# How many queued FFN steps go into each gap of the attention chunks: half of the per-chunk budget instead of a third

## The reference, cut to what matters

```python
q = elu_feature_map(proj(Wq)); k = elu_feature_map(proj(Wk)); v = proj(Wv)
# per token i, 16 heads of 64:
kv_sum = kv_sum + einsum('bhd,bhe->bhde', k_i, v_i); k_sum = k_sum + k_i
out_i  = einsum('bhd,bhde->bhe', q_i, kv_sum) / (sum(q_i * k_sum) + EPS)
x = layernorm(x + out @ Wo.T)
h = layernorm(x) * gamma + beta
y = silu(h @ dequant(fc1_q, fc1_scales) + fc1_bias)      # 1024 -> 4096
z = y @ dequant(fc2_q, fc2_scales) + fc2_bias            # 4096 -> 1024
x = layernorm(x + (x + 0.5 * z))
```

## Time and profile before

| what | value |
|---|---|
| median of 2 timed runs | 3252.29 us |
| the two runs | 3212.3 and 3292.28 us |
| the profiled execution, its time | 3161.46 us |
| its span (slowest core, core 1) | 3159.8 us |
| spans of the eight cores | 3141.0 to 3159.8 us |
| mean granted TensorE clock | 0.838 to 0.842 |
| prefix stage (to the first L690) | 521.8 us on core 1 |

### The profile page before, as it was taken

One profiled execution on the slowest core, in us unless ns is written; L12 is line 12 of the kernel. 1 busy time (PEld: TensorE's weight loads), 2 busy tenths in 40 slices (PEclk: granted clock), 3 DMA queues, 4 the chain that ended last, 5 costly groups with the idle time before them and its releaser, 6 DMA issues.

```text
span 3159.8 us, 31216 instructions; the slowest of 8 cores (3141.0 to 3159.8 us)
## 1 busy us (share of the span) xinstructions
PE 2089.2 (66%) x11268; PEld 957.4 (30%) x11268; DVE 1241.7 (39%) x1724; ACT 871.1 (28%) x1162; POOL 64.7 (2%) x126
## 2 busy tenths in 40 slices
PE   1777775666776667656765777566848674776385
PEld 0333332333332333233323333233323332333132
DVE  0555554444424432443244324334333343225314
ACT  0222222234212431143115311522152215222411
POOL 1000000000000000000000000000000000000000
PEclk9888887777798789968896889688968886888598
DMA  9677774000142113121312132321122213220241
GB/s 197 162 220 215 215 217 115 7 7 7 30 110 69 46 30 103 62 59 30 96 61 64 34 83 64 86 58 47 54 83 70 63 38 94 70 57 27 80 123 64
DMA packets 171884, 262.17 MB, mean 83 GB/s; under 512 B 40659, under 2 KB 114387, under 8 KB 169684
## 3 DMA queue, kind: packets, MB, share of 16 engines
q1 hardware_dynamic: 154164, 201.38, 22.8%
q0 software_dynamic: 17568, 58.79, 8.5%
HBM read 251.82 MB, written 33.55 MB: 90 GB/s over the span
## 4 chain that ended last, share of the span: by engine, by line
PE 48%; DVE 18%; DMA 13%; ACT 11%; issue 7%; another core or an unknown queue 2%; SPq 1%; DVEq 0%; ACTq 0%
PE PS L514 14%; PE PS L532 13%; PE PS L327 6%; DMA w1d<-wsl_a 5%; DMA w2d<-wsl_c 5%; PE PS L793 4%; DVE z_sb L543 3%; PE PS L690 3%; DMA out<-out_s 2%; DVE st_m L765 2%; ACT h_fm L472 2%; PE PS L760 2%; DVE r_s L552 1%; DVE u_s L548 1%
## 5 line engine op out<-in xcount | busy, mean ns | idle before, releaser
L532 PE MATMUL PS<-w2r_a,y_fm 128*128 128x512 bf16 x1024 | 280.0, 423 | 216.9 <-DVE z_sb L543 107.4
L327 PE MATMUL PS<-wqkv,x_fma 128*128 128x512 bf16 x1536 | 375.1, 402 | 25.7 <-DVE z_sb L543 7.1
L543 DVE TENSOR_TENSOR z_sb<-PS,z_sb 128x1024 f32<-128x1024 f32 x96 | 117.4, 1223 | 538.5 <-PE PS L532 513.4
L520 ACT ACTIVATE y_fm<-PS,b_s 128x512 bf16<-128x512 f32 x256 | 176.1, 688 | 519.0 <-PE PS L514 502.7
L514 PE MATMUL PS<-h_fm,w1r_a 128*128 128x512 bf16 x1024 | 258.9, 414 | 61.7 <-ACT y_fm L520 33.2
L532 PE MATMUL PS<-w2r_b,y_fm 128*128 128x512 bf16 x1024 | 252.9, 392 | 0.0
L514 PE MATMUL PS<-h_fm,w1r_b 128*128 128x512 bf16 x1024 | 236.7, 391 | 4.9 <-DVE st_m L765 3.0
L327 PEld LDWEIGHTS PS<-wqkv,x_fma 128*128 128x128 bf16 x1536 | 154.7, 102 | 244.3 <-issue 85.7
L532 PEld LDWEIGHTS PS<-w2r_a,y_fm 128*128 128x128 bf16 x1024 | 99.8, 105 | 383.2 <-issue 307.5
L514 PEld LDWEIGHTS PS<-h_fm,w1r_a 128*128 128x128 bf16 x1024 | 106.1, 105 | 210.0 <-issue 113.2
L711 PE MATMUL PS<-ident,khat 128*128 128x128 bf16 x256 | 27.7, 273 | 203.6 <-DVE khat L343 199.9
(11 more groups left out here) (141 smaller groups left out, 2422.0 us busy)
## 6 DMA issues: line engine op xcount, KB each, us to landing
w2r_a<-w2d SPq DMA_DIRECT2D x32, 1024.0 KB, 5.4
w2r_b<-w2d SPq DMA_DIRECT2D x32, 1024.0 KB, 7.5
out<-out_s SPq DMA_DIRECT2D x32, 512.0 KB, 2.9
s1b_a<-fc1sb SPq DMA_DIRECT2D x4, 2048.0 KB, 10.2
s2b_a<-fc2sb SPq DMA_DIRECT2D x16, 512.0 KB, 8.5
s2b_b<-fc2sb SPq DMA_DIRECT2D x16, 512.0 KB, 4.1
g1a<-fc1q POOLq DMA_DIRECT2D x4, 2048.0 KB, 11.3
g2a<-fc2q POOLq DMA_DIRECT2D x16, 512.0 KB, 5.1
```

The source lines that it names most:

```text
L327: op("tensor", lambda e, d=d, s=s, xfm=xfm: e.matmul(PS[g][:, 512 * s:512 * s + 512], xfm[:, 128 * d:128 * d + 128], wqkv[:, 3072 * d + D ...
L520: op("scalar", lambda e, m=m, lo=lo: e.activation(out=y_fm[:, 512 * (m % 8):512 * (m % 8) + 512], in_=PS0[:, lo:lo + 512], func=AF.Silu, b ...
L532: op("tensor", lambda e, m=m, s=s, rbuf=rbuf: e.matmul(PS0[:, 1024 + 512 * s:1536 + 512 * s], y_fm[:, 512 * (m % 8) + 128 * t: 512 * (m % ...
L543: op("vector", lambda e, t=t: e.tensor_tensor(out=z_sb[:, D * t:D * t + D], in0=PS0[:, 1024:2048], in1=z_sb[:, D * t:D * t + D], op=ALU.ad ...
```

## The change: half of the budget per slot

```diff
-            b3 = (budget + 2) // 3
+            b3 = (budget + 1) // 2
```

## The result

| | before | after |
|---|---|---|
| median | 3161.73 us (10 runs) | 3198.48 us (11 runs) |
| lowest to highest | 3156.63 to 3292.28 | 3191.07 to 3247.65 |
| profiled execution | 3161.46 us, span 3159.8 | 3190.32 us, span 3188.7 |
| ratio | | 1.0123, 95% interval 1.0089 to 1.0157 |
| granted clock | 0.838 to 0.842 | 0.837 to 0.841 |

The changed kernel is 1.2% slower: less than 2%, but the interval leaves out 1. The two runs of before that the prediction had (3212.3 and 3292.28) turned out to be the two highest of ten; the other eight lie between 3156.6 and 3181.6. Times as long as those two come, wherever the clock was recorded beside them, with a lower granted clock on the cores of a die (3217.3 us at 0.80, where the other die had 0.84), and such executions are left out of the ratios.

A forecast was written before the change was run, and what follows sets the result against it. The prediction took TensorE's work plus the idle stretches ahead of it as the bound. Its terms, 6.0 + 2.3 - 2.5 + 30.0 + 4.1 = +39.9 us, put on the median 3252.29, gave 3292 us, range 3195 to 3340.

The forecast's parts named there:

- round 3: Chunks 12 to 15, priced mostly by old chunks' windows: 326.7 us against 320.7, +6.0.
- round 7: Chunks 28 to 31: chunk 28 dearer, chunk 30 empty, a stall lost in 31; +4.1 us.
- Rounds 4 and 5: Each becomes the old round after it, item for item: +2.3 and -2.5 us.
- Round 6: Chunks 24 to 27, a new filling with nothing left to flush, walked slot by slot: 351.2 us against 321.2, +30.0.
- upper bound: Chunks 24 to 27 at old chunk 22's ratio to flush prices, 1.19: 356.6 us, so +35.
- fc2 pair at the start of the flush: Chunk 15's flush: first two fc2 take 10.1 + 6.4 us instead of 2 x 5.15, as z_sb waits behind layer norm.
- first fc1 of the flush: Chunk 15: leaves old chunk 15's flush, saving 13.9 us, as it waited behind the layer norm's ScalarE work.
- 1.5 because no flush lies ahead of final_block: Start of chunk 28: with no flush ahead to cover final_block's start, the chunk takes 1.5 us more.
- Rival 1: Filling slots pays: 21 FFN items leave the flushes, each hiding 1.8 us; -37 us, 3215; chance 0.08.
- Rival 2: It cancels: chunks 24 to 27 pay flush prices, +5, chunks 28 to 31 give nothing; +11 us, 3263; chance 0.17.
- Rival 3: 1 MB loads come 5.4 us late at six places, chunks 24 to 29: +72 us, 3324; chance 0.20, shared with longer VectorE chains.
- Whole rounds don't gain: TensorE's granted clock: single chunks gain from denser work, rounds 3 to 6 of before do not (0.85, 0.84, 0.84, 0.83).

The follow-up runs named there:

- round-6-only: Kernel before, with the new rule for items per slot used in chunks 24 to 27 alone; ratio to the kernel before 1.0101.
- all-but-round-6: Changed kernel, but chunks 24 to 27 keep the old rule for items per slot; ratio to the kernel before 1.0028.
- aligned kernel: Kernel before, re-dealt: each round's first chunk takes ten steps, the next three one FFN quarter each, the last quarter flushed; ratio 0.9587, repeated 0.9545.
- last experiment: Aligned kernel with one transposed h_fm tile moved from slot 4 to slot 5 in each round's first chunk; ratio to the kernel before 0.9423.
- last-quarter run: Changed kernel, but the last four fc2 of chunks 24 to 27 stay queued for the flush; ratio to the kernel before 1.0099.

## Why the prediction was right and where it was wrong

**The level was wrong, and that made the number wrong.** The failed step is "The two timed runs ... lie above that execution, with a median of 3252.29. I put the sum on the median: 3292 us". The sum of the steps on the profiled execution was 3201; the median measured is 3198.48, and the profiled execution after took 3190.32. The two timed runs at hand were the two highest of ten, and the kernel before has a median of 3161.73, within 0.3 us of its profiled execution. Against that, 3292 reads as +4.1%, which nothing in the working supports. The durations all came from the profiled execution, so the sum belonged on its time; three values spread over 4% (3161, 3212, 3292) with the profiled one lowest were a sign that time had been added to the other two, not taken from the first.

**The change was right in size and place.** +39.9 us, 1.2%, against a ratio of 1.0123 and +34 to +37 in the rounds. The total is closer than its parts by luck: round 3 was 5.0 us too low and round 7 5.9 too high, and they cancel.
- Rounds 4 and 5: item for item the old rounds 5 and 6; 323.7 and 321.2 predicted, 323.5 and 320.9 measured. Where every chunk of a round had an old one with the same content, its windows gave the time to 0.3 us.
- Round 6: +30.0 predicted, +28.1 measured; no chunk of it is off by more than 1.7 us. The round-6-only run puts the loss there, and holding the last quarter back shows its part, 7 us. Of the upper bound one step was wrong: the 22.6 us of old chunk 22 hold the 4.4 that it inherited from chunk 21; without them the ratio is 0.96 and not 1.19, and no bound above the flush prices comes of it.
- Round 3: +6.0 predicted, +11.0 measured. The mis-sized terms are small ones: chunk 12 67.2 for 66.7, chunk 13 51.3 for 50.1 (at a granted 0.83, where old chunk 14 had 0.90), chunk 15 152.5 for 149.2. In chunk 15 the fc2 pair at the start of the flush took 10.4 + 7.7 for 10.1 + 6.4. In old chunk 28, where the pair was read, it had taken 10.1 + 6.65, the second item at a granted 0.77; here that item had 0.66. The first fc1 of the flush, taken out at 13.9, had taken 13.5 in old chunk 15 (13.9 was chunk 11's). And L793 was through 1.1 us later than walked: the two fc1 of slots 1 and 3 took 9.9 and 8.9 us, for 9.4 and 8.5 in old chunk 22.
- Round 7: +4.1 predicted, -1.8 measured. Chunk 28 took 156.7, not 160.4: "1.5 because no flush lies ahead of final_block" had the wrong sign. Its first tile is transposed 33.9 us into the chunk, where it was 36.3 in old chunk 28 (2637.4 - 2601.2), 2.4 earlier. Two other runs agree: with the same content, chunk 28 takes 158.7 us on the mean of the cores where round 6 keeps its flush (all-but-round-6), and 156.7 where it has none; and in the round-6-only run the flush before it is gone and it takes 113.2, for 114.7 before. Which work of the flush had delayed it was not separated; its first transpose waits for ScalarE's u_bf_a in both traces, 22.96 us and 25.29 before.

**The rivals.** Rival 1 (filling pays) was wrong for this change, and right for another arrangement: the aligned kernels gain 4 to 6% by filling the same slots. What differs is which item lands in which slot. Rival 2 is outside the interval's lower end (1.0089 against 11 us, 1.0035). Rival 3 did not come: among TensorE's waits in the trace after there is none of L514 or L532 for a load. The outcome is the one that had 0.77, "within 2%".

**The clock.** "Whole rounds don't gain" held for this change: 0.83, 0.84, 0.83 and 0.81. It does not hold in general. The aligned kernel's round 3 runs at 0.87 and its cores at 0.854 to 0.863, where before had 0.838 to 0.842; its chunk 13 does what old chunk 25 did at 0.95 instead of 0.89, and takes 62.8 instead of 64.6.
The Trainium skill, "TensorE: Matmul & The Clock Gate", section "Why this matters for your kernels", says that idle gaps between bursts of matmuls cost clock. The trace agrees where the idle really goes, as in the last experiment's L793 (6.3 us at 0.57 against 3.6 at 1.00); for a change that only moves idle about, the clock of the rounds stayed at 0.81 to 0.84.

The section on the time before says that the clock is 1.0 or 0.5 at any moment. That holds for its trace. Six cores of two later runs, cores 4 to 7 in round-6-only and 2 and 3 in the last-quarter run, show a third level as well, 0.81, in stretches that add up to 78 to 169 us a core.

**What stays open.** Why the aligned kernel gains some 30 us more than walked is only partly the clock: the 1.8 us of chunk 13 would be 13 us over seven rounds. In round 3 of core 1 the other chunks give 1.3 and 1.2 us more than walked, and round 7 gives 8 us more; these were not separated. The prefix stage's 5.8 us between the two profiled executions are not explained either; no instruction of it changed, and they lie within what the other traces show for it.

## What to carry to other kernels

When work is dealt into gaps of a dependent chain, the amount per gap matters less than what waits there: an item that waits for the same thing as the chain hides nothing (fc2 in slot 1), and one that puts work on the engine the chain needs costs more than in the flush (the last quarter ahead of qp_tm); one that does neither is almost free (the second fc1 of chunk 25, a tile beside L793). Look up the best-filled stretch in the trace, see why it is good, and repeat it; here that gave 4 to 6%, while the two settings of the divisor are 1.2% apart. And a sum made of durations from one execution belongs on that execution's time.

## What the runs showed that had not been expected

Moving two kinds of item ahead of the same layer norm had opposite results: fc1 gave back 8 us where the next chunk followed (15.3 to 6.9 in slot 5 of chunk 24, on the mean of the cores) and 1.4 where a flush did, fc2 nothing (an idle of 2.69 before L690 in place of a stall in the K/V projection). The same sequence of matmuls took 62.8 us in one kernel and 64.6 in another, with a granted clock of 0.95 and 0.89.
